# A graph attention layer: accumulation banks that rotate from head to head, and head results one unit later on VectorE

## The reference, cut to what matters

```
h = (x @ W).reshape(n, H, C)
e = leaky_relu((h*a_src).sum(-1)[src] + (h*a_dst).sum(-1)[dst], 0.2)
ee = exp(e - segment_max(e, dst)[dst])
alpha = ee / segment_sum(ee, dst)[dst]
out = segment_sum(alpha * h[src], dst) + bias     # layer 1: H=4, C=192; layer 2: H=2, C=96
```

## Time and profile before

| | us |
|---|---|
| median of 3 runs | 1096.62 (1095.16 to 1097.81) |
| the profiled execution | 1096.85 |
| its span | 1095.0 |
| TensorE matmuls busy | 941.7 (86%) |
| VectorE busy | 774.3 (71%) |
| ScalarE busy | 343.9 (31%) |
| layer 1's units, first matmul to last | 572.7 to 720.2 of the span |

### The profile page before, as it was taken

The page is one execution under the profiler, slowest core; times in us unless marked ns, Lnnn a source line. Parts: engine busy times, 40 slices in busy tenths (PEclk is TensorE's granted clock), DMA queues, the critical chain, the costliest instruction groups (busy, mean ns, idle before and its releaser), DMA issues.

```text
span 1095.0 us, 16944 instructions
## 1 busy us (share of the span) xinstructions
PE 941.7 (86%) x6241; PEld 680.0 (62%) x6241; DVE 774.3 (71%) x1738; ACT 343.9 (31%) x424; POOL 134.6 (12%) x139
## 2 busy tenths in 40 slices
PE   3789999976968989988979889975887659999994
PEld 2766666653534446545759889865885536666662
DVE  6468789983666588787669877959997954444442
ACT  3561122202213522332324333313434722222220
POOL 3010000000000000000000000000331034555541
PEclk9789999987989999999999999997989869999997
DMA  7340222144252537546769210003208667777761
GB/s 231 117 159 15 74 73 73 59 155 149 74 197 79 204 117 256 163 129 212 235 228 415 85 48 1 1 1 136 124 1 291 238 202 196 190 188 190 187 164 20
DMA packets 61451, 155.44 MB, mean 142 GB/s; under 512 B 11940, under 2 KB 31270, under 8 KB 58426
## 3 DMA queue, kind: packets, MB, share of 16 engines
q1 hardware_dynamic: 48586, 112.33, 29.3%
q0 software_dynamic: 9936, 34.23, 12.5%
q10 hardware_dynamic: 2848, 7.77, 1.8%
HBM read 108.34 MB, written 48.94 MB: 144 GB/s over the span
## 4 chain that ended last, share of the span: by engine, by line
PE 63%; DVE 22%; DMA 6%; issue 4%; ACT 3%; SPq 1%; DVEq 1%; POOLq 0%; ACTq 0%
PE PS L1762 39%; PE PS L2005 13%; DVE arena L1505 3%; PE PS L1838 3%; DVE arena L1461 3%; DVE arena L1467 2%; PE PS L2156 2%; PE PS L1818 1%; DMA arena<-in_L_mix_Wq_dram 1%; DVE arena L1477 1%; DMA arena<-in_L_gnn_W_dram 1%; DVE arena L1367 1%; PE PS L1849 1%; DVE arena L1223 1%; DMA arena<-as_d 1%
## 5 line engine op out<-in xcount | busy, mean ns | idle before, releaser
L1762 PE MATMUL PS<-arena 128*128 128x384 f16 (+7 forms) x3396 | 568.2, 323 | 4.8 <-DVE arena L1752 3.0
L1762 PEld LDWEIGHTS PS<-arena 128*128 128x128 f16 (+2 forms) x3396 | 322.0, 99 | 216.9 <-issue 17.3
L2005 PE MATMUL PS<-arena 128*128 128x193 f32 (+1 forms) x1200 | 191.4, 323 | 21.9 <-DVE arena L1467 16.6
L2005 PEld LDWEIGHTS PS<-arena 128*128 128x128 f32 x1200 | 186.9, 200 | 26.4 <-DVE arena L1467 16.0
L1033 ACT ACTIVATE arena<-arena,AS 128x1280 f32<-128x1280 f32 x60 | 81.8, 1363 | 134.9 <-DVE arena L1461 134.7
L1461 DVE SCALAR_TENSOR_TENSOR arena<-arena,AS 128x1280 f32<-128x1280 f32 x60 | 94.2, 1573 | 0.0
L1467 DVE SCALAR_TENSOR_TENSOR arena<-arena 128x1280 f32<-128x1280 f32 x60 | 90.6, 1509 | 3.0 <-PE PS L2005 3.0
L1275 DVE TENSOR_SCALAR arena<-arena 128x240 f16<-128x240 f16 x324 | 89.3, 276 | 0.0
L1274 DVE TENSOR_SCALAR arena<-arena 128x128 f16<-128x128 f16 x324 | 80.3, 248 | 0.1
L1751 DVE SCALAR_TENSOR_TENSOR arena<-PS,arena 128x768 f32<-128x768 f32 x27 | 25.9, 958 | 62.8 <-PE PS L1762 62.8
L1838 PE MATMUL PS<-arena 128*128 128x240 f16 x324 | 45.9, 274 | 28.1 <-DVE arena L1267 28.1
(11 more groups left out here) (267 smaller groups left out, 920.6 us busy)
## 6 DMA issues: line engine op xcount, KB each, us to landing
arena<-in_L_ffn_W_dram SPq DMA_DIRECT2D x48, 384.0 KB, 3.8
fr_d<-arena SPq DMA_DIRECT2D x48, 384.0 KB, 3.5
arena<-fr_d SPq DMA_DIRECT2D x16, 1152.0 KB, 14.6
arena<-in_x_dram SPq DMA_DIRECT2D x18, 384.0 KB, 5.6
arena<-rr_d SPq DMA_DIRECT2D x4, 1280.0 KB, 8.3
g_d<-arena SPq DMA_DIRECT2D x10, 388.0 KB, 2.3
acc_d<-arena SPq DMA_DIRECT2D x10, 384.0 KB, 2.6
xf_d<-arena ACTq DMA_DIRECT2D x10, 384.0 KB, 3.3
```

What stands on the lines that cost most here:

```text
L1762: m = T.matmul(out, left[i][x], right[i][y], start=first and i + r == 0, stop=last and 3 * i + r == n - 1)
L2005: m = T.matmul(ps[b][:, r * (C + 1):(r + 1) * (C + 1)], PT[i % deep][:, d * P:(d + 1) * P], feats, start=t == 0 and r == 0, stop=t == NT - ...
```

## The change

The bank of pair `b` in head `h` of layer 1 becomes `(5h + b) % 8`: head 0 uses banks 0 to 4, head 1 banks 5, 6, 7, 0, 1, head 2 banks 2 to 6, head 3 banks 7, 0, 1, 2, 3. TensorE waits for the last release of each bank it starts: for pairs 3 and 4 those are pairs 0 and 1 of the head before; for pairs 0 to 2, from head 2 on, pairs 2 to 4 of the head two before; for pairs 0 to 2 of head 1 there is none. `head_result` of layer 1 stands behind `weights(10h+1)` in place of `weights(10h)`. Where a head's banks wrap from 7 to 0 (heads 1 and 3) its reciprocal is issued in two pieces. Layer 2 keeps banks 0 to 4 and its order.

```diff
+        def sum_bank(h, b):
+            return (5 * h + b) % 8
             def head_result(h, C, unit0):
                 dve.wait_ge(s_agg, unit0 + (h + 1) * NT)
-                acc = PS[:, 0:5 * 512].rearrange("p (a b) -> p a b", a=5)
-                link(V.reciprocal(rden[:, :, :], acc[:, :, C:2 * C + 2:C + 1]))
+                acc = PS.rearrange("p (a b) -> p a b", a=8)
+                first = sum_bank(h, 0) if C == CW else 0
+                n = min(5, 8 - first)
+                for b0, b1, a in ((0, n, first), (n, 5, 0)):
+                    if b0 < b1:
+                        i = V.reciprocal(rden[:, b0:b1, :], acc[:, a:a + b1 - b0, C:2 * C + 2:C + 1])
+                link(i)
                 for d in range(NT):
                     b, r = divmod(d, 2)
-                    v = acc[:, b, r * (C + 1):r * (C + 1) + C]
+                    v = acc[:, (first + b) % 8, r * (C + 1):r * (C + 1) + C]
...
-                    if t == 1 and h:
+                    if t == 2 and h:
                         head_result(h - 1, CW, 0)
...
                     if t == 0 and r == 0 and h:
-                        pe.wait_ge(s_head_out, 5 * (results + h - 1) + b + 1)
-                    m = T.matmul(ps[b][:, r * (C + 1):(r + 1) * (C + 1)], ...
+                        if C != CW:
+                            pe.wait_ge(s_head_out, 5 * (H1 + h - 1) + b + 1)
+                        elif b >= 3:
+                            pe.wait_ge(s_head_out, 5 * (h - 1) + b - 2)
+                        elif h >= 2:
+                            pe.wait_ge(s_head_out, 5 * (h - 2) + b + 3)
+                    m = T.matmul(ps[sum_bank(h, b) if C == CW else b][:, r * (C + 1):(r + 1) * (C + 1)], ...
```

More of the change, by code:

```diff
@@ L1997, in _, with aggregate @@
                     mixed_part(t, c0, 0, KC)
-            def aggregate(unit, i, t, h, C, deep, results, feats):
+            def aggregate(unit, i, t, h, C, deep, feats):
                 pe.wait_ge(s_p_ready, unit + 1)
@@ L2003, in aggregate @@
                     if t == 0 and r == 0 and h:
-                        pe.wait_ge(s_head_out, 5 * (results + h - 1) + b + 1)
-                    m = T.matmul(ps[b][:, r * (C + 1):(r + 1) * (C + 1)], PT[i % deep][:, d * P:(d + 1) * P], feats,
+                        if C != CW:
[4 more added lines that the diff above has]
+                            pe.wait_ge(s_head_out, 5 * (h - 2) + b + 3)
+                    m = T.matmul(ps[sum_bank(h, b) if C == CW else b][:, r * (C + 1):(r + 1) * (C + 1)], PT[i % deep][:, d * P:(d + 1) * P], feats,
                                  start=t == 0 and r == 0, stop=t == NT - 1, skip_group_check=True)
@@ L2014, in _ @@
                     pe.wait_ge(s_sel_ready, 8 if t < 2 else 9 if t < 5 else 10)
-                aggregate(i, i, t, h, CW, 3, 0, G4[:, t, h, 0:CW + 1])
+                aggregate(i, i, t, h, CW, 3, G4[:, t, h, 0:CW + 1])
             def logit_row(h, n):
@@ L2061, in _ @@
                 h, t = divmod(i, NT)
-                aggregate(H1 * NT + i, i, t, h, C2, 2, H1, h2x[:, t, h, :])
+                aggregate(H1 * NT + i, i, t, h, C2, 2, h2x[:, t, h, :])
                 if i == 0:
```

## The result

The changed kernel takes 1082.60 us (median of 4 runs, 1078.62 to 1086.84) against 1097.21 before; the ratio is 0.9866 (95% interval 0.9835 to 0.9897). Six further runs of it, in the last group of experiments, gave 1082.89 (1081.03 to 1086.25) and 0.9868 (0.9844 to 0.9893). The forecast was 1083.0. One of the four runs of before took 1299.87 us, for a reason that isn't known; it counts in the median of 1097.21 (1096.62 without it) and not in the ratio. The others lie from 1095.16 to 1097.81.

A forecast was written before the change was run, and what follows sets the result against it. TensorE was taken to bound layer 1, at 3.27 us a unit plus boundary stops and clock falls. The sum 1096.85 - 14.0 + 0.2 + 0.1 = 1083.15 gave a forecast of 1083.0 us, range 1080.0 to 1087.6.

The forecast's parts named there:

- The two stops: TensorE's stops at layer 1's head boundaries, 1.18 us for an empty bank and 1.86 us for weights, would go.
- The clock: The granted clock's falls behind the restarts of heads 1 and 2 would go, winning some 4 us.
- The 14.0 us: What can go in heads 1 to 3: 112.0 us together, against 98.0 for thirty units at 3.27 us.
- Rival (b): The clock falls in layer 1 nevertheless, 1.7 to 2.0 us twice, total 1086.8 us; chance 0.08.
- Just in time: At each boundary the third unit's weights come as TensorE needs them, 6.46 us against 6.53; 0.2 us of stops in all.
- The account of a head: A layer 1 head costs VectorE 32.2 us and TensorE 32.7, so TensorE stays the bound by 0.5 us.
- rival (c): VectorE becomes the bound: head result 1 us longer beside busy TensorE, 2.5 us in all, total 1085.5 us; chance 0.08.
- The second reciprocal: Splitting the reciprocal of heads 1 and 3 costs 0.1 us each.
- Rival (a): Banks still hold TensorE, as pair 3 or 0 waits for VectorE: 3.8 us back, total 1086.8 us; chance 0.06.
- the 0.8 us of slack: In head 1's first unit, TensorE reaches pair 3 at 610.15; pair 0 of head 0 is released by 609.37.
- (d): Remaining short stops leave the clock at its lower level for long; one whole head would give 1116 us; chance 0.02.
- (e): The change does nothing, as the weights for unit 11 still come late: 1096.6 us; chance 0.02.

The follow-up runs named there:

- the last group of experiments: On one chip: the changed kernel again, 1082.89 us; head result in two pieces with 20 unread matmuls ahead of layer 1, 1081.11; also 4 behind head 3, 1081.01.
- filling the stops: Kernel before, with unread matmuls in TensorE's two stops at each boundary (three before a head's first unit, five before its second): 1091.97 us, ratio 0.9968.
- the result in two pieces: Changed kernel with the head result split: reciprocal and pairs 0 to 2 behind the second weights, pairs 3 and 4 behind the third: 1082.79 us, ratio 0.9857.
- the longer result: Changed kernel with two further unread VectorE operations of 128x640 behind each of the first three head results: 1092.46 us, one run.
- one unit later: Changed kernel with the head result one unit later again, behind the third weights: 1085.38 us, one run; layer 1 136.25 us.

## Why the prediction was right

**The two stops.** Right, and shown apart. The position alone takes away the stop for weights (147.53 to 137.56, with the clock falls). The banks take away the one for the empty bank, but only when the weights are there to follow: alone they move it. The stops were the earlier trace rows added up; the walk through the earlier trace rows, VectorE's wait of 1.8 us in place of 4.96 and the head result starting when it did before, came out at 1.70. Their price was a little higher than I took it: with the clock up, a head with both stops takes 36.22 us against 32.67, so 3.55 us a boundary in place of some 3.2.

**The clock.** Right. The 14.0 us counted some 4 for falls; filling the stops, with the rest left as it was, gave back 3.36 in heads 1 to 3 (112.01 to 108.65), 1.68 a fall. So the two terms of the 14.0 were 10.65 and 3.36. Rival (b) did not appear: in both profiles of the changed kernel the clock is 1.00 through all boundaries. The Trainium skill, "TensorE: Matmul & The Clock Gate", section "HAM oscillation — how this bites in real kernels", puts the fall down to idle stretches longer than the stops here. These traces don't agree with that as a bound: the clock fell behind stops of 1.18 and 1.86 us with a unit between them, and once behind a single one of 1.86.

**Just in time.** The mechanism was right and the size off. I took 0.2 us for all stops at the third units; by the length of the heads they are 0.28, 0.32 and 0.28 us, 0.9 in all. The weights came when I said: ready 6.45 us behind the reciprocal (602.41 to 608.86), 6.46 said. What I left out is the weight load ahead of a unit's first matmul. With the result in two pieces the 800 loads of layer 1 run without a gap; here the load stood still for 0.31 us, until 608.92, though the weights came before 608.94, where by my own account (602.41 + 6.53) unit 11's matmuls end. The two pieces brought the weights 1.3 us earlier and removed exactly this.

The account of a head, 32.2 us on VectorE against 32.7 on TensorE, was right as a sum, but the 0.5 us between them are no cover. They lie ahead of the reciprocal, where VectorE has to wait for TensorE (0.71 us in heads 1 and 2, near 0.4 said), and behind it every delay reaches TensorE: the longer result turned all of its added 1.84 us into a stop. So rival (c), that VectorE's head result comes to hold TensorE, has the right mechanism and too low a price: a microsecond more would cost a whole one a boundary, 3 us in all, where it said 2.5. Its condition did not come: beside busy TensorE the ten operations still take 3.34 us, as before.

**The second reciprocal.** 0.1 taken. From the reciprocal's start to the first scaling it is now 0.29 us for head 1 and 0.31 for head 3, against 0.26 unsplit: 0.03 and 0.05. Head 1's shows at the boundary behind it, as said: the stop there is 0.32 us, 0.28 at the others.

**Rival (a)** (TensorE stops at pair 3): not seen, as the 0.8 us of slack suggested; it is what happens one unit later, where the release comes late and costs 0.6 us a head. **Rivals (d) and (e)** did not appear. The row loads, too, stayed covered: no wait of VectorE in layer 1 ends with a DMA.

**The total.** In heads 1 to 3 the sum said 14.0 less 0.2; they went from 112.0 to 98.9, 13.1 less. The difference of 0.7 is the stops at the third units. Layer 1 took 134.22 us, under the 138 that I had set as the mark of being wrong. The profiled execution came to 1081.04 where the sum said 1083.15. That it came below the sum is luck and not the sum's merit: 5.62 us came from the stages ahead of layer 1, whose code is the same, and 2.46 went behind head 3. I put the spread of the stages behind at 2 to 3 us each way and named the clock. The stages ahead spread more: over the thirteen profiles layer 1's first matmul comes between 567.1 and 576.8 us. That goes in part with the clock: in windows of 50 us up to 550, what it lacks of 1.00 adds up to some 21 us in the profile of after, 27.5 in that of before and 31 in the latest one. The medians, over 10 runs of after, are 14.6 us below those of before; layer 1 accounts for 13.0 to 13.3.

## What to carry to other kernels

Where an engine must wait for another to finish a stage (here VectorE for the end of a head), the wait costs least once it has handed over as much work as the buffers hold, and no later. Moving the wait one step and freeing the banks that it guards are two halves, and each has to be priced with the other absent. When a stop goes, compare what is late next in tenths of a microsecond: just in time for an operation isn't just in time for the weight load before it. Spare time that lies ahead of the wait is no cover for what comes behind it. Two stops of TensorE within a few microseconds can cost a third loss, the clock, as large as one of them; matmuls in the stops that nobody reads tell the two apart.

## What the runs showed that I had not expected

- The granted clock fell behind 3.3 us of stop in three of three, behind 1.2 and 1.9 us with a unit between them in two of three, behind a single 1.9 us in one of three, and behind a single 1.2 us in none of three (kernel with the position alone). A fall inside a head cost 1.65 to 1.68 us. What picks out the cases isn't shown.
- Unchanged code ahead of layer 1 differs by up to 9.8 us from execution to execution, in part with the clock, so that an effect under 2 us can be read from the stage in the profile and hardly from the medians.
